# Attention in one megakernel: the next pair's query chunks in steps 0, 2, 4 and 6 in place of 0 to 3

## The reference, cut to what matters

```python
q = (x @ wq).reshape(b, s, H, QH)            # per head 128 plain and 64 rotary columns
q_pe = rope(q_pe, cos, sin); k_pe = rope(k_pe, cos, sin)
scores = einsum('bhqd,bhkd->bhqk', qs, ks) * scale
attn = softmax(where(causal, scores, min))
out = einsum('bhqk,bhkd->bhqd', attn, v)
```

## Time and profile before

| | us |
|---|---|
| median of 3 runs | 1459.19 |
| lowest and highest | 1459.08, 1462.78 |
| the profiled execution | 1459.05 |
| its span in the trace | 1457.2 |
| granted TensorE clock over the span | 0.93 |

### The profile page before, as it was taken

The page is one execution under the profiler, slowest core; times in us unless marked ns, Lnnn a source line. Parts: engine busy times, 40 slices in busy tenths (PEclk is TensorE's granted clock), DMA queues, the critical chain, the costliest instruction groups (busy, mean ns, idle before and its releaser), DMA issues. The chain is left out here.

```text
span 1457.2 us, 18876 instructions
## 1 busy us (share of the span) xinstructions
PE 1227.6 (84%) x5880; PEld 881.1 (60%) x5881; DVE 844.7 (58%) x1551; ACT 626.2 (43%) x1069; POOL 961.9 (66%) x700
## 2 busy tenths in 40 slices
PE   6974699999992489988998897689889998998797
PEld 5863455555551356666666666556666666666686
DVE  4578522222224667766676654767766776673567
ACT  3220233333320245565565564135655565565242
POOL 2025768888875457877788776557876787776454
PEclk9986799999995789999999998779999999999899
DMA  9348335555555000000000000000000000002001
GB/s 327 118 153 216 98 60 82 82 80 81 80 79 167 8 8 8 8 1 8 8 8 1 1 1 12 8 8 8 8 1 8 8 8 1 1 1 64 1 8 51
DMA packets 66509, 68.28 MB, mean 47 GB/s; under 512 B 15072, under 2 KB 59680, under 8 KB 66304
## 3 DMA queue, kind: packets, MB, share of 16 engines
q1 hardware_dynamic: 48336, 43.42, 10.0%
q0 software_dynamic: 15168, 20.72, 9.2%
q10 hardware_dynamic: 2928, 3.15, 0.7%
HBM read 46.17 MB, written 21.10 MB: 46 GB/s over the span
## 5 line engine op out<-in xcount | busy, mean ns | idle before, releaser
L1512 POOL TENSOR_TENSOR att_prob_lo<-att_prob,att_prob_hi 128x1024 fp32r<-128x1024 f32 (+1 forms) x160 | 346.7, 2167 | 114.1 <-ACT att_prob_hi L1448 114.0
L1555 DVE TENSOR_REDUCE att_peak<-all_bank 128x1 f32<-128x512 f32 (+3 forms) x384 | 207.4, 550 | 208.8 <-PE all_bank L1343 140.4
L1359 PE MATMUL all_bank<-att_q_hl,sequence_k_hl 128*128 128x512 f32 (+1 forms) x960 | 263.6, 385 | 0.0
L1382 PE MATMUL all_bank<-att_prob_hi,sequence_v_hl 128*128 128x512 f32 (+1 forms) x640 | 201.6, 396 | 35.3 <-POOL att_prob_lo L1512 19.1
L1441 ACT ACTIVATE att_prob<-all_bank 128x1024 f32<-128x1024 f32 (+1 forms) x160 | 150.6, 941 | 175.9 <-PE all_bank L1365 174.7
L1359 PEld LDWEIGHTS all_bank<-att_q_hl,sequence_k_hl 128*128 128x128 f32 x960 | 170.0, 192 | 26.1
L1340 PE MATMUL all_bank<-sequence_k_hl,att_q_hl 128*128 128x512 f32 (+3 forms) x384 | 171.0, 449 | 8.7 <-DVE att_peak L1555 8.3
L1448 ACT CAST att_prob_hi<-att_prob 128x1024 fp32r<-128x1024 f32 (+1 forms) x160 | 154.2, 964 | 5.1
L1327 PE MATMUL all_bank<-sequence_x_hl,sequence_w_hl 128*128 128x512 f32 x384 | 115.0, 438 | 46.3 <-DVE all_xT L1550 38.7
L1489 POOL TENSOR_TENSOR all_xT<-all_xT 128x512 f32<-128x512 f32 x64 | 82.4, 1288 | 106.1 <-DVE all_xT L1550 105.7
L916 PE MATMUL all_bank<-early_w_gu,moe_xgT 128*128 x316 | 148.9, 554 | 3.6 <-issue 2.4
(11 more groups left out here) (244 smaller groups left out, 2103.6 us busy)
## 6 DMA issues: line engine op xcount, KB each, us to landing
sequence_w_raw<-wqk_rows SPq DMA_DIRECT2D x16, 256.0 KB, 2.7
early_w_gu<-in_gate SPq DMA_DIRECT2D x16, 224.0 KB, 5.7
early_w_gu<-in_up SPq DMA_DIRECT2D x16, 224.0 KB, 5.8
early_w_down<-in_down SPq DMA_DIRECT2D x1, 3584.0 KB, 19.8
sums<-early_zero SPq DMA_DIRECT2D x18, 128.0 KB, 3.7
all_xT<-in_xT SPq DMA_DIRECT2D x4, 512.0 KB, 7.6
all_x_tok<-in_x SPq DMA_DIRECT2D x1, 2048.0 KB, 16.3
x_rows<-all_x_tok SPq DMA_DIRECT2D x4, 512.0 KB, 3.0
```

What stands on the lines that cost most here:

```text
L1359: nc.tensor.matmul(ps, k_hl[:, ks, j * P:(j + 1) * P], q_hl[n % 2][:, qs, :, i * BW + q0:(i + 1) * BW], start=g == 0, stop=False)
L1382: mm = nc.tensor.matmul(out, v_hl[:, vs, j, :], part[:, u % 3, half * WIDE:half * WIDE + 2 * w].rearrange("p (h m) -> p h m", h=2), start= ...
L1512: nc.gpsimd.tensor_tensor(prob_lo[:, u % 3, 0:w], prob[:, u % 2, 0:w], prob_hi[:, u % 3, 0:w].bitcast(F32), ALU.subtract).then_inc(lo_sb, 1)
L1555: nc.vector.tensor_reduce(peak[:, n % 2, part, t // 2, h, t % 2:t % 2 + 1], piece_ps[y % 2][:, 0:w], AX_X, ALU.max).then_inc(peak_sb, 1)
```

## The change

The query chunks 0 to 3 of the next pair go to steps 0, 2, 4 and 6. Pieces are dealt anew: 16 of a pair's 24 while the pair before runs, in its steps 4 to 9, and 8 in its own steps 0 to 3, now for pair 0 as for the others. Reciprocals, quotients and the next weights' split move to other steps. The order inside a step stays as it was on every engine.

```diff
-    NEXT_PIECES = [0, 0, 1, 2, 3, 3, 3, 3, 3, 3]
-    OWN_PIECES = [2, 1] + [0] * (NG - 2)
-    FIRST_PIECES = [3, 3, 2] + [0] * (NG - 3)
-    EARLY = NP - sum(FIRST_PIECES)
-    INVERT_AT = {1: (-1, 0), 2: (-1, 1), 3: (0, 0), 4: (0, 1), 5: (1, 0), 6: (1, 1), 7: (2, 0), 8: (2, 1)}
-    PRODUCT_AT = {3: -1, 5: 0, 7: 1, 9: 2}
+    QUERY_AT = {0: 0, 2: 1, 4: 2, 6: 3}
+    NEXT_PIECES = [0, 0, 0, 0, 1, 3, 1, 3, 4, 4]
+    OWN_PIECES = [2, 3, 2, 1] + [0] * (NG - 4)
+    EARLY = NP - sum(OWN_PIECES)
+    INVERT_AT = {0: [(-1, 0)], 1: [(-1, 1)], 3: [(0, 0), (0, 1)], 5: [(1, 0)], 7: [(1, 1)], 8: [(2, 0)], 9: [(2, 1)]}
+    PRODUCT_AT = {0: -2, 2: -1, 4: 0, 8: 1}
...
-        out = [("query", n + 1, x)] if n + 1 < PAIRS and x < QC else []
+        out = [("query", n + 1, QUERY_AT[x])] if n + 1 < PAIRS and x in QUERY_AT else []
...
                     if made:
-                        q_high(n + 1, x)
+                        q_high(n + 1, QUERY_AT[x])
                     if x in last_of:
                         sums(n, last_of.index(x))
-                    if x == 4 and n + 2 < PAIRS:
+                    if x == 7 and n + 2 < PAIRS:
                         weights_high(n + 2)
...
-                        if 1 <= x <= QC:
-                            q_low(n + 1, x - 1)
-                        if x < QC:
-                            rotate(n + 1, x)
+                        if x - 1 in QUERY_AT:
+                            q_low(n + 1, QUERY_AT[x - 1])
+                        if x in QUERY_AT:
+                            rotate(n + 1, QUERY_AT[x])
...
-                    if x == 5 and n + 2 < PAIRS:
+                    if x == 8 and n + 2 < PAIRS:
                         weights_low(n + 2)
                     if x in PRODUCT_AT and n * NB + PRODUCT_AT[x] >= 0:
                         product(n * NB + PRODUCT_AT[x])
+                product(PAIRS * NB - 2)
```

More of the change, by code:

```diff
@@ L1253, in phase_attention @@
     block_needs = [1 + max(y for y in range(NP) if pieces[y][0] // 2 == i) for i in range(NB)]
-    NEXT_PIECES = [0, 0, 1, 2, 3, 3, 3, 3, 3, 3]
-    OWN_PIECES = [2, 1] + [0] * (NG - 2)
-    FIRST_PIECES = [3, 3, 2] + [0] * (NG - 3)
-    EARLY = NP - sum(FIRST_PIECES)
-    INVERT_AT = {1: (-1, 0), 2: (-1, 1), 3: (0, 0), 4: (0, 1), 5: (1, 0), 6: (1, 1), 7: (2, 0), 8: (2, 1)}
-    PRODUCT_AT = {3: -1, 5: 0, 7: 1, 9: 2}
+    QUERY_AT = {0: 0, 2: 1, 4: 2, 6: 3}
[4 more added lines that the diff above has]
+    PRODUCT_AT = {0: -2, 2: -1, 4: 0, 8: 1}
     def aside(n, x):
-        left = NP - sum(FIRST_PIECES if n == 0 else OWN_PIECES)
-        own = FIRST_PIECES if n == 0 else OWN_PIECES
-        out = [("query", n + 1, x)] if n + 1 < PAIRS and x < QC else []
-        out += [("piece", n, left + sum(own[:x]) + a) for a in range(own[x])]
+        out = [("query", n + 1, QUERY_AT[x])] if n + 1 < PAIRS and x in QUERY_AT else []
+        out += [("piece", n, EARLY + sum(OWN_PIECES[:x]) + a) for a in range(OWN_PIECES[x])]
         if n + 1 < PAIRS:
@@ L1471, in _ @@
                     n, x, _, _ = at(u)
-                    made = n + 1 < PAIRS and x < QC
+                    made = n + 1 < PAIRS and x in QUERY_AT
                     if u + AHEAD < STEPS:
@@ L1600, in _ @@
                         beside(item)
-                    if x in INVERT_AT:
-                        i, half = INVERT_AT[x]
+                    for i, half in INVERT_AT.get(x, ()):
                         if n * NB + i >= 0:
```

## The result

The changed kernel takes 1530.76 us (median, 1528.62 to 1532.21) for 1459.13: a ratio of 1.0487, 95% interval 1.0462 to 1.0512. The direction was forecast, the size was not: +72 us against +47 at a range that ended at 1520.

What follows compares the result with a forecast made beforehand. PE was taken to set the time through both attention stretches. Steps at full clock added 22.3 us to 1459.05, giving 1481.4; clock falls added 25 us, for a forecast of 1506 us, range 1477 to 1520.

Steps and rivals of the forecast that it cites:

- steps at full clock: All pairs and batch ends without the clock term: 12 x 1.65 + 1.9 + 0.6 = +22.3 us, giving 1481.4.
- falls of the clock: PE drops to half clock after two in three of the 28 long waits, 1.35 us each: +25 us.
- The two value waits have one cause: PE's waits before values of steps 1 and 3 (0.8, 1.3 us) both end with ACT's `sums`, queued behind q_high.
- Parts 1 to 4: One pair's four PE stretches: 10.03 + 1.70 + 10.28 + 27.0 = 49.0 us for 47.38, +1.65 us a pair.
- Ends of a batch: Pair 0 costs +1.0 us (+0.9 in batch 0); the last pair, with five more pieces, +0.3 us.
- Other engines: Steps 4 to 9: moved rope, rotate and q_high make no new wait; upper bound 0.4 us a pair, 5 in all.
- part 1: Step 0 to the values of step 1: still 10.03 us, wait 2.86 us start to start, nothing won or lost.
- The clock: Waits of 2.7 and 3.0 us a pair make PE's clock fall: +25 us; ends none, or 42.
- The clock holds: Rival: steps as forecast, but PE's clock does not fall: 1481 us, range 1476 to 1487; chance 0.23.
- Falls after the longer wait only: Rival: clock falls only after step 3's 3.0 us wait, 14 x 1.35 = +19 us, 1500 us; chance 0.13.
- Faster: Rival: POOL's `low` ends step 3's value wait, which goes with the query waits: -2.1 us a pair, 1430; chance 0.06.
- It cancels: Rival: step 1's wait is over 1.3 us shorter because ACT reaches `sums` sooner: 1456 to 1463 us; chance 0.04, with smaller things.

Runs made afterwards that it cites:

- e8: Changed kernel with POOL's `low` waiting for DVE's spread in steps 2 and 9, and 16 and 20 unused matmuls before the values of steps 1 and 3: 1476.99 us.
- e6: Changed kernel, ACT's order kept, with POOL starting `low` in steps 2 and 9 only when DVE's spread is done: 1518.3 us.
- e1: Changed kernel with ACT making a block's four copies (`sums`) before q_high instead of behind it: 1465.29 us, ratio 1.004.
- e7: Changed kernel with the queries in steps 1, 3, 4 and 6 instead of 0, 2, 4 and 6, ACT's order kept: 1436.12 us.
- e4: Changed kernel with 12 unused 256-column matmuls on PE before the values of steps 1 and 3 of each pair but the last: 1496.85 us.
- e5: Changed kernel with ACT's `sums` before q_high and POOL's `low` waiting for DVE's spread in steps 2 and 9: 1403.61 us, ratio 0.963.
- e2: Kernel before the change, with ACT making the `sums` copies before q_high: 1454.42 us, ratio 0.998.

## Why the prediction was wrong, point by point

| term | forecast | measured | from |
|---|---|---|---|
| steps at full clock | +22.3 | +18.4 | e8 less its kernel before |
| spread beside POOL's `low` | none | +12.5 | changed kernel less e6 |
| falls of the clock | +25 | +41.3 | e6 less e8 |
| sum | +47 | +72 | |

The measured terms are differences of medians of kernels that ran at different times, so each is good to some 2 us.

- *The two value waits have one cause, `sums` behind q_high.* Right. e1 moves the copies alone and both waits go, e7 moves the queries alone and both go, e6 has the view name ACT for both.
- *Parts 1 to 4.* Right to 0.15 us in each stretch, as e8 shows in isolation: the chains stay at their length, the work that filled the waits goes to where PE is never idle. The loss of 1.5 us a pair, and the direction, rest on this.
- *Ends of a batch.* Too low. Steps 0 to 3 of the last pair of batch 0 took 14.41 us and take 16.56 us (first step at 894.35, fifth at 910.91), +2.15 where I took +0.3. In e8, without the slow spread, they take 15.0 us.
- *Other engines.* This is one of the two steps that failed. I wrote that the wait for block 3's maxima is covered and counted the instructions of the spread "as long" as a maximum, 0.69 us. And part 1 took the chain to the values of step 1 to stay at 10.03 us. The spread takes 2.8 us when it meets `low`, and by the changed dealing block 2's spread stands behind the last piece of step 9, where POOL starts the `low` of that step. The rows of before that would have told me were there, spreads of 1.44 us among ones of 0.69 us, and I took no note of them since they lay where DVE had time:

```profile
694.11 1.44 DVE L1568 SCALAR_TENSOR_TENSOR att_minus<-all_bf,att_peak 128x512 bf16<-128x512 bf16 x1
...
699.88 0.69 DVE L1568 SCALAR_TENSOR_TENSOR att_minus<-all_bf,att_peak 128x512 bf16<-128x512 bf16 x1
```

It is worth 0.85 us (10.93 for 10.09 us to the values of step 1) in each of the 12 pairs behind a batch's first, and 1.5 us at each end of a batch (16.56 for 15.0): 13 us by the traces, 12.5 by the medians.

- *The clock.* The other one. The mechanism was right: e4 and e8 put work into the waits and the time falls. The term was mis-sized: "two waits in three to cost 1.35 us: 18.5 x 1.35 = +25 us", with 42 as its upper end. There were 23 falls for 28 waits, six of double length, so as many as 29 single ones for the 18.5 that I took; each cost 1.4 us (41 / 29), near the 1.35 that I took. It is the number that was too low. And the range did not carry this upper end through: 1481 and 42 is 1523, over the 1520 that I gave, before the missed term.
- *The rivals.* "The clock holds" fell with PEclk 0.93. "Falls after the longer wait only" fell as well: the window from 799.10, with the wait of 2.56 us, is followed by one at 0.50, as all 14 of the shorter waits are, while 5 of the 14 longer ones have no fall; and e1's falls follow a wait of 1.96 us. "Faster" needed POOL to be the releaser in step 3, and e1 and e6 show that it was not. "It cancels" had no row and got none.

## What to carry to other kernels

Before moving work off a wait, ask what ends the wait: if it is a chain on other engines that the move leaves alone, the wait only grows by what is moved out of it, and the work is paid again where the engine was full. Here the chain ran through an in-order queue in which the urgent copies stood behind one instruction that waits for three engines; changing their order was worth 65 us, and the changed kernel, 72 us behind with the wrong order, then came out 54 us ahead of the kernel before once POOL also kept clear of the spread (how much of that the kernel before would gain from the same two remedies is open). Price long waits of TensorE with the clock that they lose, and read every instruction's shortest and longest duration against what POOL was doing.

## What the runs showed of the hardware

- The 128x512 DVE instruction with two SBUF tensors that starts while a POOL instruction runs ends 0.54 to 0.56 us after that instruction ends, 1.2 to 2.8 us (0.9 at the least, before) in place of 0.69, in bf16 and fp32 alike; one of 128x4 that is still at work then ends 0.02 us after it (before). Where POOL stood idle 0.84 us for the spread, nothing on PE waited for that (e5).
- PE's clock fell to the level of 1.2 GHz after waits of 2.56 and 3.14 us in 23 of 28 cases, after 1.96 us in 12 of 14 (e1), after 2.1 us in 9 of 12 (e2), after 1.82 us in 8 of 14 (e4), and after 0.73 and 0.93 us, one close behind the other, in 3 of 14 pairs (e7). No fall began in the 14 pairs of the kernel before, with waits of 0.4 to 1.3 us, nor in those of e8 with waits of 0.8 and 0.95 us. So the length of the wait alone does not decide. One fall costs 1.57 us where PE sets the time.
- A profile's releaser can be an instruction that merely ends at the same moment; the order in which the program needs things, and the constant 0.14 to 0.15 us behind the true one, told them apart.
